# Last stages of a two-layer decoder: new instruction orders on five engines, and two rounding steps on another engine

## What is computed

```python
x = x + _L0_ffn_ref(_layernorm(x), ...)           # routed block: its result is scattered back to the tokens
x = x + _L1_attn_ref(_layernorm(x), weight_qkv, weight_proj)   # grouped-query attention, 16 heads, over the 4 sequences
x = x + _L1_xattn_ref(_layernorm(x), ctx_2048)    # product with a weight, both rounded to fp8 by blocks of 128
x = x + _L1_ffn_ref(_layernorm(x), w1, w2, w3)    # silu(a @ w1) * (a @ w3) @ w2, activations rounded to int8,
                                                  # weights to -1, 0, 1
# act_quant: scale = 127 / max|x|;  clip(round(x * scale), -128, 127) / scale
```

## Time and profile before

| | us |
|---|---|
| median of 3 runs | 1161.15 |
| the runs | 1160.86 to 1164.18 |
| the profiled execution | 1161.08 |
| its span, first to last instruction | 1159.4 |
| of this, last stages (from the end of the routed block, 773.2) | 386 |
| PE busy / DVE / ACT / POOL over the span | 1044.8 / 855.3 / 606.0 / 464.5 |

### The profile page before, as it was taken

How to read it: one execution, slowest core, us unless ns; L and a number is a source line. 1 busy time by engine, 2 the same in 40 slices (tenths; PEclk the granted TensorE clock), 3 DMA queues, 4 the chain that set the end, 5 groups by cost and what they waited for, 6 DMA issues and landing times.

```text
span 1159.4 us, 14674 instructions
## 1 busy us (share of the span) xinstructions
PE 1044.8 (90%) x4830; PEld 746.7 (64%) x4830; DVE 855.3 (74%) x1615; ACT 606.0 (52%) x1201; POOL 464.5 (40%) x727
## 2 busy tenths in 40 slices
PE   5789999999999999879999689997788999899796
PEld 3667887888778888644545377765556666666342
DVE  5677766776677666726776658776779999989974
ACT  4634444444434443135556547553457877777662
POOL 5344324332433233325778214113544544535420
PEclk9899999999999999989999889998889999999899
DMA  8200000000000000063010044500001112111123
GB/s 297 86 1 1 1 1 1 1 1 1 1 1 1 1 1 6 32 254 118 29 37 1 1 162 147 193 24 1 1 5 22 40 29 52 27 37 43 31 54 87
DMA packets 48427, 52.92 MB, mean 46 GB/s; under 512 B 34528, under 2 KB 35552, under 8 KB 46048
## 3 DMA queue, kind: packets, MB, share of 16 engines
q1 hardware_dynamic: 48352, 51.99, 14.0%
HBM read 39.92 MB, written 4.19 MB: 38 GB/s over the span
## 4 chain that ended last, share of the span: by engine, by line
PE 48%; DVE 21%; POOL 14%; issue 9%; ACT 5%; DMA 1%; DVEq 0%; POOLq 0%; ACTq 0%
PE bank L403 37%; PE bank L488 3%; PE bank L411 3%; DVE cum_h L901 2%; POOL pv L2323 2%; PE bank L479 1%; POOL wq L2239 1%; DVE at L1359 1%; DVE o L1389 1%; POOL wq L2243 1%; PE bank L469 1%; POOL wq L2249 1%; DVE fm L1472 1%; DVE half_lo L1235 1%; POOL wq L2232 1%
## 5 line engine op out<-in xcount | busy, mean ns | idle before, releaser
L403 PE MATMUL bank<-win_hi,a_uT_hi 128*128 128x512 f32 (+1 forms) x320 | 130.1, 407 | 7.3 <-DVE win_lo L852 4.0
L403 PE MATMUL bank<-win_lo,a_uT_hi 128*128 128x512 f32 (+1 forms) x320 | 122.3, 382 | 0.0
L403 PE MATMUL bank<-win_hi,a_uT_lo 128*128 128x512 f32 (+1 forms) x320 | 122.0, 381 | 0.0
L2125 POOL TENSOR_TENSOR y<-y,off 128x512 f32<-128x512 f32 x24 | 37.8, 1573 | 113.8 <-DVE off L922 113.8
L1603 ACT ACTIVATE ex<-bank 128x48 f32<-128x48 f32 x16 | 3.3, 209 | 150.8 <-PE bank L447 150.8
L403 PEld LDWEIGHTS bank<-win_hi,a_uT_hi 128*128 128x128 f32 x320 | 62.5, 195 | 22.0 <-issue 6.4
L403 PEld LDWEIGHTS bank<-win_lo,a_uT_hi 128*128 128x128 f32 x320 | 62.6, 196 | 13.4 <-issue 2.9
L403 PEld LDWEIGHTS bank<-win_hi,a_uT_lo 128*128 128x128 f32 x320 | 62.1, 194 | 11.9
L403 PE MATMUL bank<-wq,eT 128*128 128x512 f32 x128 | 63.5, 643 | 4.9 <-ACT eT L1897 4.6
L488 PEld LDWEIGHTS bank<-xs,wgt 128*128 128x128 f32 x512 | 61.2, 192 | 6.8 <-issue 5.7
L403 PE MATMUL bank<-f,fqT_next 128*128 128x512 fp8e4 (+1 forms) x312 | 64.0, 362 | 1.3 <-DMA fqT_next<-fq 1.3
(11 more groups left out here) (335 smaller groups left out, 3046.1 us busy)
## 6 DMA issues: line engine op xcount, KB each, us to landing
wchunk<-w_in SPq DMA_DIRECT2D x32, 256.0 KB, 5.0
stage<-f_in SPq DMA_DIRECT2D x4, 1408.0 KB, 5.9
x<-x_in SPq DMA_DIRECT2D x16, 256.0 KB, 6.0
land<-win_in SPq DMA_DIRECT2D x4, 1024.0 KB, 7.6
wq<-ctxT_in SPq DMA_DIRECT2D x4, 1024.0 KB, 8.3
ctx<-ctx_in SPq DMA_DIRECT2D x4, 1024.0 KB, 5.7
out<-x SPq DMA_DIRECT2D x16, 256.0 KB, 2.7
first_stage<-f_in SPq DMA_DIRECT2D x2, 1408.0 KB, 14.2
```

The lines of the kernel that those rows point to most:

```text
L403: made = e.matmul(bank, a, b, start=start and n == 0, stop=stop and n == len(pairs) - 1)
L2125: e.tensor_tensor(y[m % 2][:, cols], y[m % 2][:, cols], off[:], ALU.add).then_inc(sig("y_off"), 1)
```

## The change

1. `f_quantise` and `h_quantise` leave DVE's program and become ACT instructions (`ACT.Copy` with a bias of -MAGIC). The limit to 127 is gone with them.
2. Scatters and `add_routed` lie over seven turns: 4 in turn 0 and 2 in each of turns 1 to 6.
3. `wproj_hi` moves from ahead of ACT's turns to its turn 3 (ACT's first step for a tile is now in its turn 7, so nothing of ACT lies ahead of it); `wproj_lo` moves from ahead of POOL's turns to its turn 8, after the norm steps of tiles 0 and 1. The second half of `wqkv_lo` moves behind DVE's first four `add_routed`.
4. The last pass of the routed block signals each sequence's accumulator by itself, and DVE makes each `blk` on its own signal.
5. Each engine's list of a turn is new. The lag stands behind each step; 7 turns are taken off all lags of ACT's and POOL's new lists, so that they compare with DVE's:
   - PE before: scatter, attend_out 5, f_up 8, qkv 3, turn_eu 6, turn_o 4, e_product 6, turn_du 2, f_down 10. After: e_product 6, turn_o 4, f_down 10, scatter, attend_out 4, f_up 7, qkv 2, turn_eu 5, turn_du 1.
   - DVE after: add_routed, f_scale 6, f_gate 7 (part 0), f_gate 7 (1), attend_add 3 (first), f_gate 7 (2), attend_add 3 (second), h_scale 7, e_scales 4, attend_scores 2, add_to_x of e 5, low_oT 3, low_du 1, attend_softmax 2, add_down 9, add_to_x of the attention 3, attend_weights 2, e_fp8 4.
   - ACT after: f_round 6, e_centre 4, f_quantise 6, keep_qkv 2, h_round 7, high_oT 3, high_du 1, scale_eu 4, square of f 5, f_centre 5, exp_keys 2, h_quantise 7, square of e 3, square of d 0, silu 6 (two parts), scale_eu 4, silu 6 (third), d_normal 0, keep_eT 4.
   - POOL after: minus_mean 0, 5, 3 (of d, f, e), deviation of f 5, attend_part 2, deviation of d 0, attend_begin 2, attend_part 2, deviation of e 3, attend_part 2, attend_last 2, f_gains 5, attend_odd 1, h_gain 8, e_back 3.
   - SP before: turn_hq 9, store 11, turn_fq 7. After: turn_fq 6, store 9, turn_hq 7.

```diff
+        scattered_by = [0, 4, 6, 8, 10, 12, 14, 16]
...
-                made.then_inc(sig("down_done"), 1)
+                    if f == KF - 1 or b == BATCH - 1:
+                        made.then_inc(sig("down_done"), 1)
...
-                if n < BATCH:
-                    for k in range(TPB * n, TPB * n + TPB):
-                        scatter(k)
...
+                if n < len(scattered_by) - 1:
+                    for k in range(scattered_by[n], scattered_by[n + 1]):
+                        scatter(k)
...
-            w.wait_ge("down_done", KF)
             for b in range(BATCH):
+                w.wait_ge("down_done", KF + b)
                 e.tensor_tensor(blk[b][:], banks.of["acc", b][:], b2[:], ALU.add).then_inc(sig("blk_ready"), 1)
-            low_qkv(0)
-            low_qkv(1)
...
+                if n == 0:
+                    low_qkv(0)
...
+                if n == 0:
+                    low_qkv(1)
...
+            def high_proj():
+                w.wait_ge("w_loaded", 32)
+                e.activation(wproj_hi[:], wproj[:], ACT.Copy).then_inc(sig("wproj_hi"), 1)
+
+            def f_quantise(n):
+                w.wait_ge("f_rounded", n + 1)
+                w.wait_ge("x_routed", NT)
+                if n:
+                    w.wait_ge("fq_turned", 16 * n)
+                e.activation(fq[:], fu[:], ACT.Copy, bias=-MAGIC).then_inc(sig("fq_ready"), 1)
...
+            def h_quantise(n):
+                w.wait_ge("h_rounded", n + 1)
+                if n:
+                    w.wait_ge("hq_turned", 16 * n)
+                e.activation(hq[:], f_h[n % 2][:], ACT.Copy, bias=-MAGIC).then_inc(sig("hq_ready"), 1)
...
+                if n == 3:
+                    high_proj()
...
+            def low_proj():
+                w.wait_ge("wproj_hi", 1)
+                e.tensor_tensor(wproj_lo[:], wproj[:], wproj_hi[:].bitcast(F32), ALU.subtract).then_inc(
+                    sig("wproj_lo"), 1)
...
+                if n == 8:
+                    low_proj()
```

More of the change, by code:

```diff
@@ L1494, in vector_program @@
                 t0, t1, t2, t3, t4, t5, t6, t7, t8, t9, t10, t11, t12, t13, t14, t15 = behind(n, 16)
-                if n < BATCH:
-                    for k in range(TPB * n, TPB * n + TPB):
+                if n == 0:
+                    low_qkv(0)
+                if n < len(scattered_by) - 1:
+                    for k in range(scattered_by[n], scattered_by[n + 1]):
                         add_routed(k)
-                if t3 is not None:
-                    attend_scores(t3)
+                if t6 is not None:
+                    f_scale(t6)
                 if t7 is not None:
[L1501 to L1521, removed]
+                    f_gate(t7, 0)
+                if n == 0:
+                    low_qkv(1)
+                if t7 is not None:
+                    f_gate(t7, 1)
                 if t3 is not None:
@@ L1524, in vector_program @@
                 if t7 is not None:
-                    f_gate(t7, 0)
+                    f_gate(t7, 2)
+                if t3 is not None:
+                    attend_add(t3, 2)
+                if t7 is not None:
+                    h_scale(t7)
+                if t4 is not None:
+                    e_scales(t4)
+                if t2 is not None:
+                    attend_scores(t2)
+                if t5 is not None:
+                    add_to_x(t5, "e", "crossed", d_mv[2][t5 % 2], "f", "x_crossed")
+                if t3 is not None:
+                    low_oT(t3)
+                if t1 is not None:
+                    low_du(t1)
+                if t2 is not None:
+                    attend_softmax(t2)
+                if t9 is not None:
+                    add_down(t9)
+                if t3 is not None:
+                    add_to_x(t3, "attended", "attended", d_mv[1][t3 % 2], "e", "x_attended")
+                if t2 is not None:
+                    attend_weights(t2)
+                if t4 is not None:
+                    e_fp8(t4)
                 if 1 <= n < 3:
                     ternary_part(2, QUARTERS - 3 + n)
[L1528 to L1536, removed]
         def scalar_program(e):
@@ new lines, in scalar_program @@
+                if t13 is not None:
+                    f_round(t13)
+                if t11 is not None:
+                    e_centre(t11)
+                if t13 is not None:
+                    f_quantise(t13)
+                if t9 is not None:
+                    keep_qkv(t9, 0)
+                    keep_qkv(t9, 1)
+                if n == 3:
+                    high_proj()
+                if t14 is not None:
+                    h_round(t14)
+                if t10 is not None:
+                    high_oT(t10)
@@ new lines, in scalar_program @@
+                if t8 is not None:
+                    high_du(t8)
+                if t11 is not None:
+                    scale_eu(t11, 1, "e_scales", "eu_scaled")
+                if t12 is not None:
+                    square(t12, 2)
+                    f_centre(t12)
+                if t9 is not None:
+                    exp_keys(t9)
+                if t14 is not None:
+                    h_quantise(t14)
+                if t10 is not None:
+                    square(t10, 1)
+                if t7 is not None:
+                    square(t7, 0)
@@ L2380, in gpsimd_program @@
             w.wait_ge("ternary", 3 * QUARTERS - 2)
-            w.wait_ge("wproj_hi", 1)
-            e.tensor_tensor(wproj_lo[:], wproj[:], wproj_hi[:].bitcast(F32), ALU.subtract).then_inc(sig("wproj_lo"), 1)
             for n in range(NT + 15):
```

136 lines of the change are left out of this document (49 added, 87 removed).

## The result

The median fell from 1162.66 us (4 runs, 1160.86 to 1165.31) to 1144.08 us (4 runs, 1143.70 to 1147.89). The ratio is 0.9848, 95% interval 0.9825 to 0.9872. The profiled execution took 1143.97 us with a span of 1142.1, where before it was 1161.08 and 1159.4. The forecast was 1148, with 1139 to 1160 as its range. The first lines answer and the earlier trace rows: the page after, busy time and chain shares, then the windows (busy us and instructions of PE, PEld, DVE, ACT and POOL, granted PE clock, DMA share, GB/s).

The account below looks back on a forecast made before the run. No single engine bounds the chain; in the middle PE and DVE, both within 6% of full, take turns being late. 1161.08 - 8.5 (start) - 5.4 (turns) + 1.0 (end) = 1148.2 us, taken as 1148; range 1139 to 1160.

Parts of the forecast that it names:

- the rival of 1141: Middle: PE alone is the bound, turns of 19.25 us with the start at its best; chance 0.15.
- the start: Up to the first `qkv_product`: ten us earlier by the new order, of which 8.5 kept; 3 to 10 possible.
- the turns: Middle, 860 to 1100: 12 turns at 19.7 us, 0.45 saved in each, 5.4 us in all.
- the end: Last tiles: moved roundings with nothing beside them and `turn_hq` behind a `store` cost 1.0 us, from 0.5 to 2.
- The late projection: Start, POOL: `wproj_lo`, 5.63 us, no longer stands ahead of the first tile's mean.
- The two scatters fewer ahead of `qkv_product`: Start, PE: 2 scatters left and not 4 ahead of the first `qkv_product`, 2.6 us saved.
- the eight scatters put off: Turns 3 to 6, PE: they cost 6.9 us, but PE waits for the norm there anyway.
- The move's price on ACT: Middle: the two rounding steps add 2.18 us a turn to ACT, 2.0 after overlap.
- `h_scale` near 19.7 and even from turn to turn: Middle, DVE: sign of being right, the distance from one `h_scale` to the next near 19.7 us and even.
- The short cover: Between `turn_o` and `attend_out`: only `f_down`, 2.18 us, and transposes cover 1.5 us of work; fits by 0.6, costed at nothing.
- the slower rival: Ahead of `attend_out`: `low_oT` comes late, PE stands each turn, turns of 21.1 and 1168 us; chance 0.14.
- POOL's last sum: Ahead of PE's `turn_o`: ends about 1.1 us ahead, where before PE waited 1.69; costed at nothing.

Follow-up runs that it names:

- e3: Changed kernel with both halves of the projection weight, and the second half of `wqkv_lo`, made ahead of the turns or first additions: 1145.82 us.
- e2: Changed kernel with four scatters and four additions in each of turns 0 to 3, as before: 1150.37 us.
- e6: Kernel before with its old lists but all four parts of the change (of the projection only POOL's half moves): 1156.14 us.
- e4: Changed kernel keeping only the new lists, with roundings, scatters, projection and signals as before: 1164.24 us.
- e7: Changed kernel with two of the 11 matmuls of `f_down` left out: 1140.24 us.
- e8: Changed kernel with only `f_quantise` back on DVE, behind the second `attend_add`: 1155.59 us.
- e13: Changed kernel with only `f_quantise` back on DVE, five steps later in its list, behind `attend_scores`: 1151.30 us.
- e1: Changed kernel with both `f_quantise` and `h_quantise` back on DVE: 1156.54 us.
- e5: Changed kernel with `turn_o` ahead of `e_product` in every turn: 1157.43 us.
- e12: e11 with unused matmuls in five PE waits: first `turn_du`, `turn_eu` of tiles 0, 1 and 13, last `f_down`: 1138.98 us.
- e10: e2 with two unused matmuls, as long as a scatter, put in `attend_out` where the changed kernel has scatters in turns 4 to 6: 1145.10 us.
- e11: Changed kernel with `turn_o` ahead of `e_product` in three turns of four, behind it in the fourth: 1142.62 us.

## Why the prediction was right, and where it wasn't

The time lies within the range, but nearer to the rival of 1141 than to the forecast of 1148, and its start comes out by two errors that cancel. The three terms were -8.5 for the start, -5.4 for the turns and +1.0 for the end: -12.9. Measured in the table: from the first scatter to tile 0, -8.4, and the first scatter itself -0.5; all turns from tile 0 to tile 15, -9.4; the end, +1.0. In all -17.3.

- **The start: right in its sum, wrong in its reasons.** The first mean was to be near 778 (777.81), the power 0.55, the first `qkv_product` near 784.6 (784.87), and so they are. The last of the three is luck. The step behind the power took 1.58 us, so that the norm ended at 782.3, 6.1 us earlier than before and not 7.4; and from PE's first transposes to `qkv_product` 3.6 us were saved and not 2.6 (2.52 us against 6.11), with fewer scatters and PE's clock higher in their windows (0.84 against 0.62). `wproj_lo` was covered as argued: it ended at 792.0, and tile 2's square came at 794.33, right behind the softmax. But the parts to which the 8.5 was credited don't carry it. The late projection was put at 5.6 of the 7.4 us; e3 shows 1.7, since the time comes back before tile 4. The two scatters fewer ahead of `qkv_product` were put at 2.6; e2 shows 0.85 there. The 2.6 is half of four scatters at 0.65 us a record, with the clock at 0.62 from 790 to 795, where the same prediction prices the eight put off at 0.43. And the eight scatters put off, which the prediction counted as a cost hidden in waits, are worth 6 us by e2's median, 3.5 by its profile: they keep PE working in waits and its clock up. That they fill waits was right; that a filled wait is itself worth something was missing, though the earlier trace rows had the clock at 0.83 and 0.89 there. Nor do the parts give the start by themselves: under the old lists they are worth 1.7 of the 8.4 us to tile 0 (e6), and the new lists without them nothing (e4).
- **The turns: mis-sized, 5.4 against 9.4.** Two errors. The turn was put at 19.7 and is 19.46. The lengths of turns were read from DVE's `h_scale` (20.89, 18.48), which isn't PE's pace: before, PE's turns were 20.83, 20.48 and twice 19.46. The short ones, put at 19.6, were at 19.46 already and gained nothing; the long ones lost 1.0 to 1.6 us where 1.2 was allowed, taken off DVE's 20.89. What fell away as well was DVE's standing in line with the other two, and with the new lists DVE is just short of being late at all (19.37, e7). So this is most nearly the rival that PE alone is the bound: each turn is the 0.34 for `eT` and PE's other 19.12; that rival's 19.25 lacked the wait. Here 8 turns saved 0.65 each in the mean. The rest is their number. The prediction let twelve turns save and took 860 to 1100 as the middle; tiles 0 to 4 gained another 2.8 and 12 to 15 another 1.4.
- **The move's price on ACT: right.** 1.36 and 0.62 us a tile, 1.98, against 2.0. ACT's new load was to be 69.9 of 77, that is 36.3 in 40 us; it is 35.5. DVE's was to be 37.0 and is 35.3. ACT didn't become the bound. One sign of the forecast, `h_scale` near 19.7 and even from turn to turn, didn't come: it goes from 17.70 to 20.27, while PE's turns are even. The Trainium skill's rule of "ScalarE: Activation LUTs", Rules for kernel authors, that additions belong on VectorE, holds for the instruction (0.43 against 0.62 us) and not for this kernel: e8, which follows it for one step, is 11.5 us slower.
- **What the move removes: the step that was missing.** The prediction counted DVE's instructions, and not the handover from ACT to DVE that goes with them. By the earlier trace rows it was nearly free before (4.0 and 1.8 us of idle time in 16 tiles), because the old order asked late. e8 and e13 show that it is a matter of place: 6.9 us in the middle with DVE asking early, 1.9 with it asking late, and then 5 at the end for the last tile in the one profile that there is. On ACT each of the two steps has 0.1 us of idle time ahead of it in 16 tiles. No place on DVE that is good in the middle and at the end was found here, and others weren't tried.
- **The short cover: it was put at nothing, and that holds for the full turns alone.** `attend_out` was to follow `turn_o` by 2.6 us with 0.6 to spare:

```profile
964.10 0.68 DVE L1395 TENSOR_TENSOR oT_lo<-bank,oT_hi 128x512 fp32r<-128x512 f32 x1
```

```profile
964.93 0.55 PE L405 MATMUL bank<-wproj_hi,oT_hi 128*128 128x512 f32 x1
```

  `low_oT` ends at 964.78, 0.15 us ahead of `attend_out`, and 0.15 is the distance in after wherever PE waited for it (814.83 to 814.98, for one). So in this turn and in one more of four nothing is to spare; in the other two the distance is 0.67, and 0.5 is to spare. In the filling turns the slower rival's mechanism is there in after itself, 7.45 us of waits for `oT_lo` where before had 4.64. e1, e4 and e8 show it as it was described once DVE is late: waits of 0.4 to 2.9 us in most turns.
- **POOL's last sum:** 1.1 ahead of `turn_o` by the layout, 1.9 measured (ends 999.26, `turn_o` 1001.18). e5 takes away the 3.5 us of `e_product` that lay ahead of `turn_o` and gets a wait of 2.15.
- **The end: right,** +1.0. The last two DMA waits are 1.48 and 4.88 where they were 1.28 and 4.36, and the last `f_down` is slower than the 2.54 us of other turns in both.

What stays open: why the stretch to tile 0 is 51 or 53 us in like kernels, beyond that the granted clock differs in it, and how much of e3's 1.7 us is that. That the parts and the lists give 17.6 us together, and apart a gain of 5.6 and a loss of 2.4, is measured; what ties them is traced for the roundings in the middle, and for the start it isn't. The blocks signalled singly were never tried alone; the first scatter's wait went from 0.88 to 0.38 us, and its start varies by more.

## What to carry to other kernels

Before pricing a step that moves between engines, look for the handover that moves with it: an in-order engine that asks for another's result early ties both together, and costs several times the instruction. A change of lists and one of loads may each do nothing alone, so test them together and apart. And where PE waits for about two microseconds or more, work put off into the wait, or even matmuls of no use, can pay through the clock behind it, if no other wait follows at once (e12 gained at its end and not at its start).

## What the runs showed of the hardware

- The granted clock of PE fell behind some waits of 1.9 to 4.9 us, and what came next paid: `attend_out` 5.46 us at 0.50 against 3.01 at 1.00 (e2, after); `e_product` 6.41 against 3.67 and the last `f_down` 4.60 against 2.55 (after, e12). Short bursts of unused f32 matmuls in the wait kept it up (e10, e12), and were worth about 5 us in e10 against e2 and 3.6 in e12 against e11, each by medians.
- A fall isn't certain. The same wait of 1.93 us ahead of tile 1's `attend_out` was followed by 3.01 us for its matmuls in after and by 4.58 in e13. A profile's clock in a stretch belongs to that execution.
- ACT takes 1.36 us for a copy with a bias from 1408 f32 columns to bf16 (1.47 with f32 out and a scale), and 0.62 for 512 columns (0.71).
